# A four-layer graph kernel: identity added to the diagonal blocks on GpSimd, folded biases, and set-up loads ordered by need

## The reference, cut to what matters

```python
# layer 0: attention with 4 heads over the edges adj > 0.5, then + bias
# layer 1: seven relations, maximum over them
A_list = [A, A, shifted, A^T, A^T, shifted^T, eye]      # A is adj
HW  = features @ W[r, :F]  +  W_edges[r] @ W[r, F:]     # per relation r
out = max_r(A_r @ HW_r) + b
# layer 2
A_hat = A + eye
dis   = (A_hat.sum(-1) + EPS) ** -0.5
out   = relu(mask * ((dis * A_hat * dis) @ (H @ W.T + b)))
# layer 3
xn  = layernorm(x) * gamma + beta
L   = eye - s_out * adj * s_in
out = softplus(xn @ W_self + (L @ xn) @ W_neigh)
```

## Time and profile before

| what | value |
|---|---|
| median of 3 runs | 764.88 us (763.68 to 766.92) |
| the profiled execution's own time | 766.7 us |
| its span, first to last instruction | 764.9 us |
| TensorE matmul busy | 695.8 us (91%) |
| VectorE busy | 581.3 us (76%) |
| ScalarE busy | 458.3 us (60%) |
| GpSimd busy | 301.1 us (39%) |
| mean granted TensorE clock | 0.978 of 2.4 GHz |

### The profile page before, as it was taken

The page is one execution under the profiler, slowest core; times in us unless marked ns, Lnnn a source line. Parts: engine busy times, 40 slices in busy tenths (PEclk is TensorE's granted clock), DMA queues, the critical chain, the costliest instruction groups (busy, mean ns, idle before and its releaser), DMA issues. The chain is left out here.

```text
span 764.9 us, 20772 instructions
## 1 busy us (share of the span) xinstructions
PE 695.8 (91%) x7890; PEld 569.7 (74%) x7890; DVE 581.3 (76%) x1730; ACT 458.3 (60%) x1137; POOL 301.1 (39%) x359
## 2 busy tenths in 40 slices
PE   0357999999999999999999999999999999999844
PEld 0256777969697887969697978879696979787543
DVE  1658588888888888888888888887888888786330
ACT  0174566666757676666667576766667576754332
POOL 0215163543624453545435344525445253343310
PEclk9988999999999999999999999999999999999977
DMA  7000202020200202020201002020202010000000
GB/s 207 14 2 2 70 3 70 2 83 3 79 7 9 76 2 84 2 84 2 83 3 61 24 3 84 1 85 2 84 3 83 3 53 19 15 3 15 0 15 14
DMA packets 28796, 27.84 MB, mean 36 GB/s; under 512 B 1493, under 2 KB 20506, under 8 KB 28698
## 3 DMA queue, kind: packets, MB, share of 16 engines
q1 hardware_dynamic: 25344, 25.17, 10.6%
q10 hardware_dynamic: 3354, 1.35, 0.9%
HBM read 22.31 MB, written 4.19 MB: 35 GB/s over the span
## 5 line engine op out<-in xcount | busy, mean ns | idle before, releaser
L363 POOL TENSOR_TENSOR rstd<-ve,half_neg 128x4 f32<-128x4 f32 x48 | 52.4, 1091 | 257.0 <-DVE ve L1030 161.9
L1249 PEld LDWEIGHTS ps<-part,pos 128*128 128x128 bf16 x3072 | 99.6, 98 | 3.2 <-DVE pos L942 0.7
L1249 PE MATMUL ps<-part,pos 128*128 128x66 bf16 x3072 | 101.4, 193 | 0.5 <-DVE pos L942 0.5
L947 DVE SCALAR_TENSOR_TENSOR pos<-ps,neg_s,none 128x512 bf16<-128x512 f32 x128 | 87.2, 745 | 12.5 <-issue 12.5
L1011 DVE TENSOR_REDUCE best<-ps 128x128 f32<-128x896 f32 x64 | 68.5, 1085 | 22.1 <-PE ps L1317 20.2
L608 ACT ACTIVATE side<-ps,sd 128x512 bf16<-128x512 f32 x128 | 76.8, 680 | 3.0 <-DVE pos L942 3.0
L1355 PE MATMUL ps<-y,adj_tr 128*128 128x128 f32 x512 | 70.6, 283 | 2.5 <-ACT y L512 2.5
L1355 PEld LDWEIGHTS ps<-y,adj_tr 128*128 128x128 f32 x512 | 65.0, 199 | 2.8 <-ACT y L512 2.8
L1235 PEld LDWEIGHTS ps<-part,nmask 128*128 128x128 bf16 x1536 | 53.5, 99 | 14.8 <-issue 10.5
L1393 PE MATMUL ps<-u,adj_tr 128*128 128x128 f32 x512 | 61.1, 278 | 2.5 <-ACT u L702 2.5
L1235 PE MATMUL ps<-part,nmask 128*128 128x66 bf16 x1536 | 54.7, 197 | 6.9 <-DVE part L930 6.9
(11 more groups left out here) (168 smaller groups left out, 1619.7 us busy)
## 6 DMA issues: line engine op xcount, KB each, us to landing
adj_in<-in_adj SPq DMA_DIRECT2D x16, 1024.0 KB, 6.0
x_in<-in_x SPq DMA_DIRECT2D x16, 256.0 KB, 6.4
out_y<-y_out SPq DMA_DIRECT2D x16, 256.0 KB, 6.7
w_sb<-in_L_gnn_W ACTq DMA_DIRECT2D x7, 64.0 KB, 5.1
b_sb<-in_L_gnn_b ACTq DMA_DIRECT2D x1, 256.0 KB, 8.9
c_rows<-c_parts ACTq DMA_DIRECT2D x6, 1.5 KB
w0c<-in_L_gnn_W ACTq DMA_DIRECT2D x1, 64.0 KB, 2.9
a_bc<-in_L_gnn_a_src ACTq DMA_DIRECT2D x1, 64.0 KB, 5.7
```

The costliest lines, as they stand in the source:

```text
L363: G.tensor_tensor(rstd[:], ve[:], half_neg[:, 0:T], ALU.pow).then_inc(power, 1)
L947: last = V.scalar_tensor_tensor(pos[0][:, t, :], bank(B_SPREAD[h]), neg_s[:, t, h:h + 1], none[:, t, :], ALU.is_gt, ALU.is_gt)
L1249: last = mm(ps[:, B_HEADS[q] + i // 2, o:o + VAL], pos[h % 2][:, t, i * P:(i + 1) * P], parts[n][:, t, h, :], start=False, stop=(i % 2 == ...
```

## The change

It does five things.

1. Layer 2: a new GpSimd step own_blocks adds the identity to the four diagonal blocks of the transposed adjacency, into a new tile adj_own, by four additions of 128 x 128. conv_product uses these blocks in place of the plain ones and drops its four identity matmuls. It waits for them (own_ok); own_blocks waits for the previous graph's conv_product.
2. Layer 3: ScalarE's copy of zt becomes an activation with gamma as scale and beta as shift. laplace_bias, w3_gamma and the beta rows go away; laplace_linear uses w3_both as it is.
3. Layer 1: the seventh edge row goes into b1 in the set-up and is subtracted from the other relations' rows (through additional rows of c_rows for the first four), so the second edge product has 256 columns and not 384.
4. Loads are counted by use on six semaphores and split over two queues: ScalarE's has the head weights, the small operands of the set-up and the layer 3 weights; SyncE's has features and adjacency of graph 0, features of graph 1, b1, b2, w1, then adjacency of graph 1. SyncE also issues the spreading of the edge rows, now 11 small DMAs.
5. VectorE's set-up is put in functions in the order head_weights, norm0 of graph 0, edge_rows, biases, laplace_weights. TensorE's first adjacency transposes wait until edge_rows has read PSUM.

The core of the diff:

```diff
+            load_adjacency(at(0))
+            load_features(at(1))
+            (b1_sb, b2_bc on s_conv; seven w1_sb on s_w1)
+            load_adjacency(at(1))
+            load_features(at(2))
+            sync.wait_ge(s_setup, 8)
+            (11 DMAs c_rows <- c_parts on s_rows)
@@ gpsimd
+            @of_graph
+            def own_blocks(g):
+                pool.wait_ge(adj_sb, g.all(T))
+                if g.has(1):
+                    pool.wait_ge(ay2_ps, g.before(1).all(1))
+                for t in range(T):
+                    last = G.tensor_tensor(adj_own[:, t, :], adj_tr[g.three][:, t, t * P:(t + 1) * P], ident[:], ALU.add)
+                last.then_inc(own_ok, 1)
                 add_b1(at(s - 3))
+                own_blocks(at(s - 3))
                 rstd_2(at(s - 3))
@@ scalar: order of loads w0, a_src, a_dst | edge_t, w1_edge, w2, mask | bias0 | gamma, beta, w_self, w_neigh
-                A.copy(zt[:], bank(B_XNT)).then_inc(zt_sb, 1)
+                A.activation(zt[:], bank(B_XNT), ACT.Identity, scale=gamma_c[:, 0:1], bias=beta_c[:, 0:1]
+                             ).then_inc(zt_sb, 1)
@@ vector
-            dve.wait_ge(s_const, 16 * CONST_LOADS)
+            head_weights()
+            norm0(at(0))
+            edge_rows()
+            biases()
+            laplace_weights()
@@ tensor
-            pe.wait_ge(s_const, 16 * CONST_LOADS)
+            pe.wait_ge(s_small, 16 * 4)
+            mm(ps[:, 6, 256:256 + F], edge_t[:, 6:7].broadcast_to([REL, P]), w1_edge[:, 6, :], start=True, stop=True)
-            mm(ps[:, 4, 0:2 * F], beta_c ..., w3_both ...)
@@ adjacency(0) of graph 0
+                            pe.wait_ge(s_setup, 3)
@@ relation
-                    mm(b, sum_rows[:, blk], c_rows[:, 4 * F:7 * F], start=False, stop=True).then_inc(hw_ps, 1)
+                    mm(b[:, 0:2 * F], sum_rows[:, blk], c_rows[:, 4 * F:6 * F], start=False, stop=True, ...)
@@ conv_product
+                pe.wait_ge(own_ok, g.all(1))
-                        mm(own, adj_tr[g.three][:, t, i * P:(i + 1) * P], y2[:, t, :], start=(t == 0), stop=False)
-                    last = mm(own, ident[:], y2[:, i, :], start=False, stop=True)
+                        left = adj_own[:, t, :] if t == i else adj_tr[g.three][:, t, i * P:(i + 1) * P]
+                        last = mm(own, left, y2[:, t, :], start=(t == 0), stop=(t == T - 1))
@@ layer 3
-                    mm(bank(B_LAP + a), ones_b[:], bw_rows[:].unsqueeze(1).broadcast_to([P, 2, 2 * F]), ...)   (x2)
-                              w3_gamma[:], start=False, stop=(t % 2 == 1), skip_group_check=True)
+                              w3_both[:].rearrange("p a f -> p (a f)"), start=True, stop=True)
```

More of the change, by code:

```diff
@@ L343, in _ @@
             load_features(at(0))
-            for s in range(GRAPHS + DEPTH - 1):
+            load_adjacency(at(0))
+            load_features(at(1))
+            for dst, src in (
+                    (b1_sb[:], b1.rearrange("(t p) f -> p t f", p=P)),
+                    (b2_bc[:], b2.partition_broadcast(P)),
+            ):
+                sync.dma_start(dst, src).then_inc(s_conv, 16)
+            for n, r in enumerate(ORDER):
+                sync.dma_start(w1_sb[:, n, :], w1[r, 0:F, :]).then_inc(s_w1, 16)
+            load_adjacency(at(1))
+            load_features(at(2))
+            sync.wait_ge(s_setup, 8)
+            for row in range(2 * PARTS + 1):
+                lo, hi = ((2, 4), (0, 2), (4, 6))[row // PARTS]
+                sync.dma_start(c_rows[row * PARTS:(row + 1) * PARTS, lo * F:hi * F],
+                               c_parts[0:1, :, lo * F:hi * F]).then_inc(s_rows, 16)
+            for n in range(4):
+                sync.dma_start(c_rows[2 * PARTS * PARTS:(2 * PARTS + 1) * PARTS, n * F:(n + 1) * F],
+                               c_parts[0:1, :, 6 * F:7 * F]).then_inc(s_rows, 16)
+            for s in range(2, GRAPHS + DEPTH - 1):
                 load_adjacency(at(s))
@@ L495, in _ @@
[L495 to L498, removed]
+            act.dma_start(w0c[:, 0:F], w0.rearrange("d h f -> d (h f)")).then_inc(s_heads, 16)
+            act.dma_start(a_bc[:, 0, :], a_src.rearrange("h f -> (h f)").partition_broadcast(P)).then_inc(s_heads, 16)
+            act.dma_start(a_bc[:, 1, :], a_dst.rearrange("h f -> (h f)").partition_broadcast(P)).then_inc(s_heads, 16)
@@ L499, in _ @@
+            act.dma_start(edge_t[:], w_edges.rearrange("r d -> d r"), allow_slow_non_contiguous=True).then_inc(s_small, 16)
+            act.dma_start(w1_edge[:], w1[:, F:F + REL, :].rearrange("r d o -> d r o")).then_inc(s_small, 16)
+            act.dma_start(w2_in[:], w2).then_inc(s_small, 16)
+            act.dma_start(mask_in[:], nodemask.rearrange("g (t p) -> (g t) p", p=P)).then_inc(s_small, 16)
+            act.dma_start(bias0_bc[:], bias0.partition_broadcast(P)).then_inc(s_bias, 16)
             for dst, src in ((gamma_c, gamma), (beta_c, beta)):
@@ L500, in _ @@
                 act.dma_start(dst[:], src.rearrange("(f o) -> f o", o=1), allow_slow_non_contiguous=True
[L501 to L508, removed]
+                              ).then_inc(s_lap, 16)
@@ L1099, in _ @@
                 pair(1)(at(s - 2))
-                norm0(at(s))
+                if s > 0:
+                    norm0(at(s))
                 attention(at(s - 2))
@@ L1315, in piece @@
                     mm(a, sum_rows[:, blk], c_rows[:, 0:4 * F], start=False, stop=True, skip_group_check=True)
[L1316 to L1317 removed]
+                    mm(b, h1t[:, blk], w1_sb[:, 4:7, :], start=True, stop=False, skip_group_check=True)
+                    mm(b[:, 0:2 * F], sum_rows[:, blk], c_rows[:, 4 * F:6 * F], start=False, stop=True,
+                       skip_group_check=True).then_inc(hw_ps, 1)
                 return piece
@@ L1368, in laplace_bias, with laplace_linear @@
             @of_graph
-            def laplace_bias(g):
+            def laplace_linear(g):
+                pe.wait_ge(zt_sb, g.all(1))
+                if g.n == 0:
+                    pe.wait_ge(s_w3, 1)
                 if g.follows(1):
                     pe.wait_ge(best_ok, g.after(1).all(T))
[L1372 to L1378, removed]
                 for t in range(T):
                     last = mm(bank(B_LAP + t // 2)[:, (t % 2) * 2 * F:(t % 2 + 1) * 2 * F], zt[:, t * P:(t + 1) * P],
-                              w3_gamma[:], start=False, stop=(t % 2 == 1), skip_group_check=True)
+                              w3_both[:].rearrange("p a f -> p (a f)"), start=True, stop=True)
                 last.then_inc(lap_ps, 1)
```

131 lines of the change are left out of this document (75 added, 56 removed).

## The result

The changed kernel takes 728.33 us (median of 4 runs, 727.97 to 728.84) against 765.69 us before (median of 4). The ratio is 0.9515 with a 95% interval of 0.9491 to 0.9539. Forecast were 727 us and a range of 720.5 to 741. In the profiled executions the span falls from 764.9 to 726.7 us, 38.2 us; the sum had 38.1. That the total fits so closely is partly luck: the terms in the middle hit, and those at the two ends missed by about 1.4 us each, in opposite directions.

What follows compares the result with a forecast made beforehand. TensorE's own list of work was taken to bound the middle, with waits at both ends. From the span, 764.9 - 24.2 (TensorE's work) - 13.9 (start) = 726.8 us, said as 727; range 720.5 to 741.

Steps and rivals of the forecast that it cites:

- What bounds: Whole steps in the middle: TensorE's own list of work is the time, 42.23 us a step, 40.7 after the change.
- TensorE's terms: Per step: identity matmuls 0.89 us, layer 3's bias 0.43, edge rows 0.21; in all 14.3 + 6.5 + 3.4 = 24.2 us.
- The additions: Four block additions on GpSimd behind add_b1: about 0.49 us each, 1.9 us in all, costing the kernel nothing.
- The turn-taking: GpSimd and VectorE alternate when both have something waiting, so part_lo goes first when add_b1 ends and own_blocks waits.
- the margin of 0.41 us: Between part_lo's end on VectorE and TensorE's no_edges(0): it shrinks from 0.62 us to 0.41 but holds.
- Rival D: Additions cost 1.27 us each and GpSimd keeps its turn; TensorE stalls 4.7 us in 15 steps: 797 us; chance 0.03.
- The copy of zt: ScalarE's copy becomes an activation of the same shape on the same engine; taken at nothing.
- The start: Before the first attention: new load and set-up order lets scores of graph 0 start at 26.1 us, 13.9 us earlier.
- the landing of the small loads: Loads 4 to 7 of ScalarE's queue, needed first by TensorE, land at 12.0 us (bounds 10 and 18.4).
- The rest of the chain: In the start: TensorE's set-up takes 4.3 us, then VectorE's work up to scores of graph 0 takes 9.8.
- VectorE's chain would be late next: In the start: after the change VectorE's chain itself, no longer a load, is what is late.
- Rival B: Small loads wait behind large ones; TensorE's set-up starts at 18.4 us as before, gain 7.5: 733 us; chance 0.12.

Runs made afterwards that it cites:

- after: The changed kernel itself, with nothing put back; 728.33 us.
- x_ident: Changed kernel with layer 2's four identity matmuls per graph again and without the additions on GpSimd; 743.69 us.
- x_bias: Changed kernel with two bf16 matmuls of 512 columns, adding zeros, in front of layer 3's linear part again; 733.62 us.
- x_edge: Changed kernel with the second edge-row product 384 columns wide again, the last 128 adding zeros; 731.87 us.
- x_start: Changed kernel with the edits of x_ident, x_bias and x_edge at once, leaving only the start of the change; 752.05 us.
- x_unused: Changed kernel with its identity matmuls again, the four block additions still running on GpSimd with their result unused; 744.07 us.
- x_long: Changed kernel with GpSimd's add_b1 as one addition of 1024 elements in place of 512, the second half unused; 737.13 us.
- x_split: Changed kernel with 512 unused elements as a second GpSimd instruction behind add_b1, ahead of the four block additions; 726.87 us.
- x_waitall: Changed kernel with VectorE and TensorE waiting for every weight load before their set-up, as before the change; 729.46 us.
- x_oneq: Changed kernel with all weight loads on ScalarE's queue in the same order, SyncE's only with features and adjacency; 728.41 us.
- x_late: Changed kernel with VectorE's work on edge-row parts, b1, b2 and layer 3 weights moved behind graph 0's scores; 725.10 us.
- x_best: x_late with the four small loads first on ScalarE's queue and VectorE's head weights behind its reading of the edge rows; 721.69 us.

## Why the prediction was right, point by point

**What bounds.** Right. TensorE was without a gap before, and stays so at 40.70 us a step (forecast 40.7). The thirteen steps between no_edges(0) of graph 2 and of graph 15 run from 128.10 to 677.10 before and from 114.27 to 643.31 after; each is shorter by 1.535 us, 20.0 us together.

**TensorE's terms.** 0.89, 0.43 and 0.21 us a step, forecast and measured alike (x_ident, x_bias, x_edge). They add up: x_start has 42.23.

**The additions.** At nothing, and so they are (x_unused). Estimated at 0.49 us each; the group after shows 0.44 to 0.45 for the undisturbed ones and up to 1.48 for the first of four, which waits for part_lo:

```profile
L497 POOL TENSOR_TENSOR adj_own<-adj_tr,ident x64: 444/453/1477, 68.3 to 679.4; 128x128 f32<-128x128 f32 x64
```

The turn-taking read from the earlier trace rows, and the margin of 0.41 us (measured 0.42), were the delicate step. Both hold, and x_long shows that the margin was real: part_lo ends 1.08 us later in its place in the step, which costs 0.76 us a step. The difference, 0.32 us, is the part of the margin that can be used, for in x_long no_edges(0) starts 0.10 us after part_lo's end even when it waits for nothing else. Rival D would have needed additions that hold part_lo up for 2.9 us and go first; each takes 0.45.

**The copy of zt.** A small miss. Taken at nothing, it takes 0.78 us with scale and shift where the copy took 0.59. In the steps that is hidden, as TensorE's laplace_linear comes 2 us after it ends; in the tail TensorE waits for it 0.87 us twice. Most of that wait was there before too, filled by the two bias matmuls. For graph 15, from the transposes of z to laplace_linear it is now 1.98 us (708.00 to 709.98) and was 1.79 (746.07 to 747.86), so the miss costs 0.2 us:

```profile
PE ps L1439 <- ACT zt L721: 1.7, 2, 0.9
```

**The start.** The mechanism was right and the size 1.2 us off: scores gained 12.7 us, forecast 13.9. The term that was mis-sized is the landing of the small loads, 13.5 us and not 12.0. The forecast scaled by bytes from the fifth load of the queue before, 320 KB against 344. The loads of ScalarE's queue after, with KB and us from issue to landing, say what that left out:

```profile
w_edge<-in_L_gnn_W ACTq DMA_DIRECT2D x1, 56.0 KB, 8.5
...
w_in<-in_L_gnn_W ACTq DMA_DIRECT2D x1, 64.0 KB, 7.0
...
mask_in<-in_nodemask ACTq DMA_DIRECT2D x1, 32.0 KB, 6.5
```

They are issued at 2.87, 5.29 and 6.86 us, so they land at about 11.4, 12.3 and 13.4. The fifth load landed a little ahead of the forecast's 12.0; the two behind it, which TensorE also needs, took about 1 us more each. In the ten kernels here with this order of loads TensorE's set-up starts between 13.01 (x_split) and 13.48 us (after; x_waitall, which waits for more, is left out), so 0.5 us of it is scatter. That SyncE's new weight loads ran beside them is not the reason: in x_oneq the adjacency of graph 1 runs there in their place, as before the change, and the set-up starts at 14.92. What makes a load take 6.5 to 8.5 us here is not shown.

The rest of the chain held: 4.6 us from TensorE's set-up to VectorE's first read (forecast 4.3), 9.25 to the scores (9.8). That VectorE's chain would be late next is what x_late confirms. Rival B, which lets the set-up start no earlier than before, was only a quarter true: 13.5 lies between 12.0 and 18.4. To no_edges(0) of graph 2 the sum had 15.2 us (the start's 13.9, and 1.3 for the matmuls of graphs 0 and 1 up to there); measured are 128.10 - 114.27 = 13.8.

**The tail.** Not split up in the forecast. After no_edges(0) of graph 15 its terms leave two layer 2 products, two bias products and one graph's relations: 2.9 us. Measured are 87.8 - 83.4 = 4.4. The rest is TensorE's clock in graph 15's layer 2 product, which took 6.4 us before (730.63 to 736.99) and 3.8 after (695.09 to 698.93), 2.5 us less, of which 0.9 go to the identity matmuls and 1.6 are left for the clock. The last but two of the numbers is the granted clock, before and after:

```profile
730.90:738.90 8.00, 6.09 (x40) 5.90 (x39) 1.39 (x2) 2.60 (x7) 1.28 (x1) 0.79 0.11 35
...
692.70:700.70 8.00, 5.00 (x40) 4.61 (x40) 1.30 (x3) 4.07 (x11) 1.27 (x1) 1.00 0.10 30
```

The forecast had the clock only in its range and not in its sum. The gain is no work of the change, and it made up for the 1.4 us that the start fell short: luck.

## What to carry to other kernels

Where one engine has no gap, price its instructions from start to start and check the other engines' margins at their narrowest point: here 0.4 us at one VectorE instruction decided whether 14 us were a gain. On GpSimd beside a VectorE instruction with both inputs in SBUF, several short instructions were safer than one long one, since the two took turns by instruction. In a start, ask what the first result needs and in what order each engine does its set-up: VectorE's order was worth 9 us of scores, and moving the rest of its set-up into later waits was worth 3 more. To price a microsecond or two, compare where the same instruction starts in two traces; totals here moved by as much with the clock.

## What the runs showed of the hardware that was not expected

**The clock in the tail takes 2 us either way.** With identical work on TensorE in the tail, after spends 80.0 us from its last no_edges group (start at 646.74) to the end of the span at 726.7, and x_split 78.1 (646.59 to 724.7). The granted clock (last but two of the numbers) of the stretch with graph 14's layer 2 product, after:

```profile
660.70:668.70 8.00, 6.88 (x40) 6.15 (x41) 2.33 (x14) 5.88 (x16) 2.72 (x4) 0.79 0.00 0
```

and x_split, the stretch at the same distance from the end:

```profile
658.70:666.70 8.00, 6.31 (x48) 5.48 (x48) 3.78 (x21) 5.62 (x15) 1.45 (x3) 1.00 0.00 0
```

Ahead of it TensorE had waited about 0.5 and 1.2 us for ScalarE in both. In after eight passes then take 1.77 us:

```profile
662.15 1.77 PE L1419 MATMUL ps<-y,adj_tr 128*128 128x128 f32 x8
```

and in x_split 1.06:

```profile
662.00 1.06 PE L1421 MATMUL ps<-y,adj_tr 128*128 128x128 f32 x8
```

The first is for a part at the low level of 1.2 GHz, the second wholly at 2.4 GHz. Why the clock falls in one kernel and not in the other, with the same waits ahead, these runs don't tell. It needn't be the kernel: of x_split's four runs three have a mean granted clock of 0.979 and take 726.66 to 726.93 us, and the fourth, at 0.974, takes 727.95, as long as after's four (0.973 and 0.974). It is the better part of the scatter between x_ident's span (739.1) and x_unused's (741.6), whose steps are the same, and why step lengths were used for the terms.

The start has such a place too, graph 0's layer 1 product. The same eight passes before and after:

```profile
72.20 5.28 PE L1283 MATMUL ps<-adj_tr,h 128*128 128x512 f32 x8
...
61.00 3.96 PE L1341 MATMUL ps<-adj_tr,h 128*128 128x512 f32 x8
```

They take 3.9 to 4.2 us in after, x_ident, x_edge, x_late and x_best and 4.9 to 5.6 in the others. That is 1.6 of the 3.2 us by which x_oneq was behind at graph 2.

**A shorter start made a low-clock stretch longer.** After the projection TensorE now idles 3.5 us (it waits for VectorE's scores and ScalarE's copies behind them), and its next eight transposes run at the low level. The stretch of that in after (0.50 is the granted clock):

```profile
28.00:31.00 3.00, 2.53 (x12) 2.17 (x12) 1.76 (x3) 0.33 (x2) 1.74 (x3) 0.50 0.01 2
```

In the kernel before, the idle time there was 1.3 us, and the same work ran at 1.00:

```profile
41.00:44.00 3.00, 2.51 (x19) 2.07 (x19) 2.69 (x8) 1.04 (x4) 0.32 (x1) 1.00 0.01 3
```

Of the 12.7 us at the scores 11.7 were left when attention of graph 0 began (no_edges(0) at 38.99, before at 50.68). In x_late and x_best TensorE idles 1.29 us there, as before, and this loss is gone: x_late gained 2.2 us at the scores and 3.2 in time.
